# Sixteen expert tiles gathered inside the last attention group, twelve of them computed before the last routing results are in

## The chip, the cores and the metric

One core of one Trainium2 chip runs the whole program in one launch. The metric is the device time of a run in microseconds (us). Five engines work side by side, each through its own instructions in order: TensorE (PE, matmuls into the eight banks of the accumulator memory PS), VectorE (DVE), ScalarE (ACT), GpSimd (POOL) and SyncE (SP, which only issues DMAs here). They wait for each other on semaphores.

## What is computed

The reference embeds 4096 tokens (4 batches of 1024), adds one attention block and then a mixture of experts. Only the last part matters for the change:

```python
def _moe_forward(x, moe_router, moe_w13, moe_w2):
    router_logits = jnp.einsum('td,de->te', x_flat, moe_router)
    topk_logits, topk_idx = jax.lax.top_k(router_logits, TOP_K)        # 2 of 8 experts
    topk_weights = jax.nn.softmax(topk_logits, axis=-1)
    ...
    x_sort = x_flat[token_ids_sort]                                    # tokens sorted by expert
    w13_out = jax.lax.ragged_dot(x_sort, moe_w13, group_sizes)         # 256 -> 2 * 512
    gate, up = jnp.split(w13_out, [MOE_DIM], axis=-1)
    hidden = jax.nn.silu(gate) * up
    out_dispatch = jax.lax.ragged_dot(hidden, moe_w2, group_sizes)     # 512 -> 256
    out_flat = jnp.zeros_like(x_flat).at[token_ids_sort].add(out_dispatch * w_sort[:, None])
```

The attention ahead of it has 16 heads of width 16 (`softmax(p p^T / 4) p` with one projection p for queries, keys and values), an output projection, and a layer norm before each part.

## The kernel before

**Attention.** The work is cut into 16 groups of 256 tokens, four to a batch (`GROUPS`, `LAST = 15`). A group is 64 items: an item is one 128x512 block of scores. PE writes three items at a time (a unit) into banks 0 to 2 or 3 to 5 (`scores`), ACT takes the exponential of the whole unit (L758), and PE adds four items at a time (a quad, 16 to a group) into bank 6 (`sums`, L359). Between the quads of a group PE does the small products of the group before, at places that `after(quad)` lists: `fold`, `turn`, `tile_rows` (twice, L402 and L403), `rank`. DVE works on the same group a step later: `fold_out`, `place_blocks`, `copy_rows` (which gives back bank 7 to the second `tile_rows`), `choose` (the best two experts), `rank_read_out` and `places_out` (the place of each token in the list of its expert), `normalise` and `normal_rows` (the rows for the experts), `weigh`. So in group 15 the routing of group 14 is done, and places of group 13 are handed out at its start.

**Lists.** POOL writes each token's number into the slot that `places_out` gave it, in a table in HBM (`note`, 4 DMAs a group). An expert's list is cut into tiles of 128 slots; the work is always 68 tiles of 72 possible (`USUAL`, `ETILES`).

**Between the parts.** When group 15 has been summed, its own fold, turn, rows, choice and ranks follow one after the other (L379, L386, L414, L435), then `tiles_out` on DVE (which tile belongs to which expert), `normalise(15)`, `places_out(15)`, `last_slots`, the table gather on POOL (L709), `slot_table` on PE (L419, L421), `slots_out` (`idx_tok`, the tokens of every tile), `near_out` and `flags_out`. Twelve matmuls of no use (L626) run at the end. Only then POOL gathers the rows of tile 0 (L1421) and SP transposes them (L1400).

**Expert weights.** 24 pieces of 512 KB go through three raw buffers: SP loads piece n once the low half of piece n-3 is done, POOL or ACT casts its high half (L700, L732), POOL subtracts to get the low half (L631). 19 pieces are done beside the attention (`BESIDE`); pieces 19 to 23 lie where the exponentials were, so ACT casts them only after the last sum.

**Experts.** For tile j: `up` (12 matmuls of 512 columns, L1472), silu on ACT (L1522), weight and product on DVE (`hidden`, L1553), its two bfloat16 halves (`halved`, L1558 and L1560), a DMA transpose of these (L1405), `down` (12 matmuls of 256 columns, L1481), copy on ACT (L1527), and an adding scatter by POOL (L1438). PE does down(j) and then up(j+4), in a loop of four tiles. The scatter of tile m waits for scatter m-2.

## Time and profile before

| | us |
|---|---|
| median of 3 runs | 875.73 (874.70 to 876.11) |
| span of the profiled execution | 874.2 |
| last sum of the attention ends | 541.35 |
| first up begins | 579.18 |
| first down begins | 590.67 |
| thirteenth down begins | 639.85 |

The record gives the span of the profiled execution (first to last instruction) and no time of its own around it; 874.2 is 1.5 below the median of the runs. All times below are from the start of the span. A row of the timeline is a start, a duration, an engine, a line, an operation with its output and inputs, and a count; in brackets stands how long the engine had been idle and what released it. Rows of neighbouring equal instructions are merged, so the duration of a merged row covers all of them. Line numbers are those of the kernel before; L1472 and its like are written `PE L1472`.

### The profile page before, as it was taken

The page shows a single profiled execution, that of the slowest core. Times are in us where ns is not written, and L with a number is a line of the kernel's source. Part 1 is how long each engine was busy: PE and PEld are TensorE (multiplying, and loading weights), DVE is VectorE, ACT ScalarE, POOL GpSimd, SP SyncE. Part 2 cuts the span into 40 slices and gives each one's busy share as a digit, 9 for nine tenths or more (in the row PEclk, how much of TensorE's full clock was granted, in tenths as well). Part 3 has the DMA queues.
Part 4 walks back from the last instruction along what each step waited for, and adds up shares of the span by engine and source line. Part 5 has one row for each costly group of instructions (what it writes and reads, how often), then busy time and mean ns, then how long its engine had stood idle before and what let it go on. Part 6 is the DMA issues. An engine that isn't in the chain of part 4 may idle for free.

```text
span 874.2 us, 16623 instructions
## 1 busy us (share of the span) xinstructions
PE 767.1 (88%) x5249; PEld 300.0 (34%) x5250; DVE 510.9 (58%) x1623; ACT 544.6 (62%) x515; POOL 355.0 (41%) x305
## 2 busy tenths in 40 slices
PE   3699994999999999989999997289999999999992
PEld 1233220222222222222222221135555555555551
DVE  7644563576667558676756478654555555545540
ACT  0468993999989999989999997312222222222221
POOL 6760030302411330241133217256666666666652
PEclk9589996899999999999999999579999999999997
DMA  2030105012011101201110124349999999999973
GB/s 40 2 94 1 37 12 38 13 37 74 13 37 49 46 16 37 74 14 37 49 50 14 37 73 98 87 85 166 159 162 164 158 162 163 160 163 156 154 122 44
DMA packets 141362, 67.72 MB, mean 77 GB/s; under 512 B 114822, under 2 KB 136984, under 8 KB 141294
## 3 DMA queue, kind: packets, MB, share of 16 engines
q1 hardware_dynamic: 125262, 49.33, 27.5%
q0 software_dynamic: 16032, 17.55, 13.9%
q8 instruction: 35, 0.57, 0.4%
q14 instruction: 33, 0.27, 0.2%
HBM read 22.52 MB, written 17.57 MB: 46 GB/s over the span
## 4 chain that ended last, share of the span: by engine, by line
PE 69%; DVE 16%; ACT 5%; issue 5%; DMA 2%; another core or an unknown queue 1%; POOL 0%; SPq 0%; POOLq 0%; ACTq 0%; DVEq 0%
PE PS L359 20%; PE PS L1472 18%; PE PS L1481 10%; PE PS L347 9%; ACT shared L758 5%; PE PS L402 2%; PE PS L379 2%; DVE room L788 2%; DVE room L794 2%; PE PS L403 2%; DVE room L786 2%; PE PS L445 1%; DMA room<-room 1%; DVE room L790 1%
## 5 line engine op out<-in xcount | busy, mean ns | idle before, releaser
L758 ACT ACTIVATE shared<-PS 128x1536 f32<-128x1536 f32 x342 | 464.8, 1519 | 48.5 <-PE PS L347 36.3
L359 PE MATMUL PS<-shared,va 128*32 128x512 f32 x2048 | 279.8, 619 | 5.1 <-DVE room L1245 4.7
L637 POOL DMA_INDIRECT slots<-pair_no,room x60 | 59.5, 991 | 364.3 <-DVE room L917 350.6
L1472 PE MATMUL PS<-w_p,room 128*128 x816 | 186.7, 379 | 0.0
L347 PE MATMUL PS<-room,ak 32*128 32x512 bf16 x1024 | 137.5, 394 | 14.3 <-ACT shared L758 9.5
L1522 ACT ACTIVATE shared<-PS 128x512 f32<-128x512 f32 x68 | 40.6, 598 | 162.9 <-PE PS L1472 162.9
L1438 POOL DMA_INDIRECT out<-room,idx_tok x68 | 110.9, 1631 | 67.1 <-ACT room L1527 38.6
L1553 DVE SCALAR_TENSOR_TENSOR shared<-shared,room,PS 128x512 f32<-128x512 f32 x68 | 50.8, 748 | 124.5 <-ACT shared L1522 124.5
L1481 PE MATMUL PS<-shared,room 128*128 x816 | 101.1, 273 | 8.6 <-issue 5.9
L1472 PEld LDWEIGHTS PS<-w_p,room 128*128 128x128 f16 x816 | 79.8, 98 | 82.9 <-issue 0.6
L347 PEld LDWEIGHTS PS<-room,ak 32*128 32x128 bf16 x1024 | 33.5, 91 | 215.6 <-ACT shared L758 166.8
L1421 POOL DMA_INDIRECT room<-xrows,idx_tok x68 | 71.8, 1056 | 48.6 <-issue 28.2
L1481 PEld LDWEIGHTS PS<-shared,room 128*128 128x128 bf16 x816 | 76.2, 97 | 40.8 <-issue 27.0
L359 PEld LDWEIGHTS PS<-shared,va 128*32 128x32 f32 x2048 | 40.7, 109 | 67.2 <-issue 56.0
L1527 ACT COPY room<-PS 128x256 f32<-128x256 f32 x68 | 25.3, 372 | 61.5 <-PE PS L1481 60.8
L823 DVE COPY room<-PS 128x264 f32<-128x264 f32 x32 | 13.8, 433 | 65.8 <-PE PS L403 64.0
L1560 DVE TENSOR_TENSOR room<-shared,room 128x512 bf16<-128x512 f32 x67 | 46.4, 692 | 2.3
L1558 DVE CAST room<-shared 128x512 bf16<-128x512 f32 x67 | 35.0, 522 | 2.3
L644 POOL DMA_INDIRECT cw<-coeff,xi x32 | 31.1, 971 | 10.8 <-issue 9.3
L631 POOL TENSOR_TENSOR w_p<-room,w_p 128x1024 bf16<-128x1024 f32 x16 | 34.4, 2147 | 1.4
L786 DVE CAST room<-PS 128x512 bf16<-128x512 f32 x32 | 22.0, 688 | 18.5 <-PE PS L334 18.5
L794 DVE SCALAR_TENSOR_TENSOR room<-room,part_c 128x512 bf16<-128x512 bf16 x32 | 27.6, 861 | 1.1
(283 smaller groups left out, 616.2 us busy)
## 6 DMA issues: line engine op xcount, KB each, us to landing
room<-w SPq DMA_DIRECT2D x24, 512.0 KB, 4.9
xrows<-room SPq DMA_DIRECT2D x16, 258.0 KB, 3.2
out<-room SPq DMA_DIRECT2D x16, 256.0 KB
room<-room SPq DMA_TRANSPOSE x135, 4.1
room<-xrows,idx_tok POOLq DMA_INDIRECT x68
out<-room,idx_tok POOLq DMA_INDIRECT x68
slots<-pair_no,room POOLq DMA_INDIRECT x60
xT<-xT SPq DMA_DIRECT2D x3, 256.0 KB, 4.3
```

What stands on the lines that cost most here:

```text
L347: last = pe.matmul(PS[:, WIDE * (u % BUFS) + i, :], g.ak[r, k0:k0 + P], qf[r, grp % 2, 512 * c:512 * c + 512], start=True, stop=True)
L359: last = pe.matmul(PS[32 * slot:32 * slot + 32, ACC, :], g.va[:, KT * (grp // HG) + kt, c, :], prob[:, (4 * quad + slot) % (RING * WIDE), ...
L637: pool.indirect_dma_start(g.slots, bass.IndirectOffsetOnAxis(pos_i[:, grp % 2, 2 * k + kk:2 * k + kk + 1].bitcast(U32), 0), g.pair_no[:, t ...
L758: act.activation(prob[:, at:at + n, :].rearrange("p n q -> p (n q)"), PS[:, buf:buf + n, :].rearrange("p c q -> p (c q)"), ACT.Exp).then_i ...
L794: dve.scalar_tensor_tensor(qf[:, grp % 2, 512 * half:512 * half + 512], u2[:], g.part_c[:, 1:2], ures[:], ALU.mult, ALU.add).then_inc(qf_r ...
L1421: pool.indirect_dma_start(xs_w[:, j % XBUF, :], None, g.xrows, bass.IndirectOffsetOnAxis(g.idx_tok[:, j:j + 1].bitcast(U32), 0), bounds_ch ...
L1438: pool.indirect_dma_start(out, bass.IndirectOffsetOnAxis(g.idx_tok[:, m:m + 1].bitcast(U32), 0), y_s[:, m % XBUF, :], None, bounds_check=T ...
L1472: last = pe.matmul(PS[:, up_bank(k) + half, :], xsT[:, k, 2 * a + c, :], g.w13_p[:, w, c, ds(e, 1), FF * half:FF * half + FF].rearrange("p ...
L1481: last = pe.matmul(PS[:, YB[k % 2], 0:D], hidT[:, k, 4 * a + c, :], g.w2_p[:, w, c, ds(e, 1), :].rearrange("p e d -> p (e d)"), start=n == ...
L1522: act.activation(act_s[:], PS[:, up_bank(k), :], ACT.Silu).then_inc(silu_done, 1)
L1553: dve.scalar_tensor_tensor(hid[:], act_s[:], weight[:, k % 2:k % 2 + 1], PS[:, up_bank(k) + 1, :], ALU.mult, ALU.mult).then_inc(hid_ready, 1)
L1560: dve.tensor_tensor(halves[:, k, 1], hid[:], halves[:, k, 0], ALU.subtract).then_inc(hid_split, 1)
```

## The change

The order of the lists is used: after group 13 an expert's first n tiles are full, if it has n times 128 tokens, and nothing later changes them. The first 16 such tiles (`LEAD`) become tiles 0 to 15; the rest are numbered after them, so there are still 68.

- DVE: `lead_tiles` (24 small instructions) after `places_out(13)`, `lead_copy` before and `lead_slots` after `rank_read_out(14)`. The last routing chain is interleaved with `lead_hidden(0)` to `lead_hidden(11)`, four instructions each.
- POOL: `lead_rows` (gather of the table's 16 rows, then of the rows of tiles 0 to 3) goes ahead of `note(14)`; the low halves of pieces 19 to 23 and the gathers of tiles 4 to 7 are mixed; the last table gather comes after the gather of tile 7 and scatter 0. Scatters up to the sixteenth wait for the one before.
- PE: `lead_table` at quad 11 of group 15; `up` of tiles 0 and 1 on both sides of the last quad's sum; tiles 2 and 3 between fold, turn and rows; then twelve `lead_step`s (down(j), up(j+4)) with `rank(15)`, `slot_table` and the last flag product between them. The twelve matmuls of L626 are gone.
- ACT: silu of tiles 0 to 3 between the casts of pieces 19 to 23; the activations of `last_rows` and the exponential `gap_exp(15)` after silu(5).
- SP: the transposes of tiles 0 to 3 after the loads of pieces 19 to 21; piece 22 is loaded after the transpose of hidden tile 0, piece 23 after that of hidden tile 1.
- The tile buffers take the place of keys, queries, values and tokens of batches 0 to 2. For the case that everything has to be done again these are saved to HBM in groups 12 and 13 (four DMAs, 3.2 MB).
- The loop begins at tile 12 (`FIRST`), with the next gathers from tile 16 on.

```diff
+LEAD = 16
+CUT = GROUPS - 3
+KEPT = NBATCH - 1
...
             if initial and grp == CUT - 1:
+                keep_keys()
+            if initial and grp == CUT:
+                keep_tokens()
...
+        for n in range(BESIDE, BESIDE + WB):
             load(n)
-        store_x(GROUPS - 2)
-        store_h(GROUPS - 1)
-        store_x(GROUPS - 1)
+        for j in range(XBUF):
+            tiles_of.turn_x(sp, j, 0)
+        later = iter(range(BESIDE + WB, len(pieces)))
+        for j in range(LEAD - XBUF):
+            tiles_of.turn_hidden(sp, j % XBUF, j)
+            if j == 0:
+                store_x(LAST - 1)
+            for n in later:
+                load(n)
+                break
...
+            tiles_of.turn_x(sp, j % XBUF, j // XBUF + 1)
...
+        def lead_table():
+            pe.wait_ge(lead_copied, 1)
+            pe.wait_ge(rank_read, LAST)
+            pe.matmul(PS[:, UB, 0:LEAD], lead_f[:], g.ident[0:LEAD, 0:LEAD], start=True, stop=True).then_inc(lead_turned, 1)
...
+        def lead_step(j):
+            now, coming = tiles_of.expert(pe, j), tiles_of.expert(pe, j + XBUF)
+            if j == 0:
+                pe.wait_ge(w_lo, len(pieces))
+            if j == 1:
+                pe.wait_ge(rank_read, GROUPS)
+            tiles_of.wait_hidden(pe, j)
+            tiles_of.wait_rows(pe, j + XBUF)
+            tiles_of.down(pe, j % XBUF, j, now)
+            tiles_of.up(pe, j % XBUF, j + XBUF, coming)
...
+        pe.wait_ge(w_lo, W13)
+        pe.wait_ge(lead_ready, 3)
+        pe.wait_ge(exp_done, UNITS - 2)
+        tiles_of.wait_rows(pe, 0)
+        lead_up(0)
         while quad < ITEMS // 4:
             sums(quad)
             after(quad)
             quad += 1
+        tiles_of.wait_rows(pe, 1)
+        lead_up(1)
+        fold(LAST)
         last_residuals()
-        fold(LAST)
+        tiles_of.wait_rows(pe, 2)
+        lead_up(2)
         turn(LAST)
+        tiles_of.wait_rows(pe, 3)
+        lead_up(3)
         last_rows()
+        lead_step(0)
         rank(LAST)
+        for j in range(1, 6):
+            lead_step(j)
         slot_table()
+        lead_step(6)
+        lead_step(7)
...
-        for n in range(12):
-            pe.matmul(PS[:, 0, :], g.ones_b[:], g.ak[:, 0:512], start=True, stop=True)
+        for j in range(8, LEAD - XBUF):
+            lead_step(j)
...
+        def lead_rows():
+            for k in range(2):
+                pool.wait_ge(noted[k], 64 * ((CUT + 2 - k) // 2))
+            pool.wait_ge(lead_row_ready, 1)
+            pool.indirect_dma_start(lead_s[:], None, g.table,
...
+            for j in range(XBUF):
+                tiles_of.gather(pool, j)
...
             if grp == LAST:
+                lead_rows()
             if grp >= 1:
                 note(grp - 1)
-        for n in range(BESIDE, BESIDE + WB):
+        for n in range(BESIDE, len(pieces)):
             low(n)
+            if n == BESIDE:
+                tiles_of.lead_gather(pool, XBUF)
+            if n == BESIDE + 2:
+                tiles_of.lead_gather(pool, XBUF + 1)
+        for j in range(XBUF + 2, 2 * XBUF):
+            tiles_of.lead_gather(pool, j)
...
         act.wait_ge(summed, ITEMS // 4)
         act.wait_ge(w_hi, BESIDE)
-        for n in range(BESIDE, BESIDE + WB):
+        for j in range(XBUF):
+            high(BESIDE + j)
+            tiles_of.silu(act, j, j)
+        for n in range(BESIDE + XBUF, len(pieces)):
             high(n)
...
+        for j in range(LEAD - XBUF):
+            if j == 2:
+                last_rows()
+                gap_exp(LAST)
+            tiles_of.copy_y(act, j % XBUF, j)
+            tiles_of.silu(act, j % XBUF, j + XBUF)
```

On PE the end of group 15 stands so in the kernel before: L347 is `scores`, L359 `sums`, L408 the residual rows, L379 the fold, L386 the turn.

```order
L347 MATMUL PS<-room,ak 128x512 [waits exp_done]
L359 MATMUL PS<-shared,va 32x512 [waits exp_done]
L359 MATMUL PS<-shared,va 32x512 x3
L359 MATMUL PS<-shared,va 32x512 [waits exp_done]
L359 MATMUL PS<-shared,va 32x512 x3
L408 MATMUL PS<-resid,xT 128x264 x2
L379 MATMUL PS<-fold_sel,room 128x64 [waits rank_read,u_read,acc_copied]
```

The same place in the changed kernel, where L388 is `scores`, L400 `sums`, L1601 the load of the tile's expert and L1614 `up`:

```order
L388 MATMUL PS<-room,ak 128x512 [waits exp_done]
L400 MATMUL PS<-shared,va 32x512 [waits exp_done]
L400 MATMUL PS<-shared,va 32x512 x3
L1601 TENSOR_LOAD tile_expert [waits exp_done,xT_in0,lead_ready,w_lo]
L1601 ISA x2
L1614 ISA [waits hid_ready]
L1614 MATMUL PS<-w_p,ak 128x512
```

The last quad's sum, which came right behind the other, now stands behind the whole first `up`, and this waits for the transposed rows of tile 0.

On DVE, what follows `normal_rows(14)` in the changed kernel: L1401 copies the sums of group 15, L1641 to L1651 are the four instructions of a `lead_hidden`, L1051 to L1053 are `weigh(14)`, L908 and L912 `fold_out(15)`.

```order
L1401 TENSOR_SCALAR room<-PS 128x512 [waits a_summed]
L1641 TENSOR_SCALAR xq<-second,xq 128x1 [waits xT_in0]
L1644 SCALAR_TENSOR_TENSOR shared<-ak,xq,PS 128x512 [waits silu_done,weighed]
L1649 CAST xT<-shared 128x512 [waits hid_ready]
L1651 TENSOR_TENSOR xT<-shared,xT 128x512 [waits split_step]
L1051 TENSOR_SCALAR room<-room 128x2 [waits gap_done]
L1052 RECIPROCAL room<-room 128x2 [waits p_dve_step]
L1053 SCALAR_TENSOR_TENSOR room<-room 128x2 [waits p_dve_step]
L908 RECIPROCAL room<-PS 128x32 [waits folded]
L912 TENSOR_TENSOR room<-PS,room 128x4x16 [waits rden_step]
```

Before, the fold's instructions stood right behind the copy; now a `lead_hidden` and `weigh(14)` are between.

On SP the tail of the changed kernel: L268 loads a weight piece, L1565 transposes gathered rows, L1570 transposes a hidden tile, L278 stores rows.

```order
L268 DMA room<-w2 128x4x256 x3
L1565 DMA_TRANSPOSE ak<-xq 128x4x128 x4
L1570 DMA_TRANSPOSE va<-xT 128x8x128
L278 DMA xrows<-room 128x2x258
L268 DMA room<-w2 128x4x256
L1565 DMA_TRANSPOSE ak<-xq 128x4x128
L1570 DMA_TRANSPOSE va<-xT 128x8x128
L268 DMA room<-w2 128x4x256
```

Before, all five loads stood together ahead of every transpose; now the last two stand behind transposes of hidden tiles.

## Rows read from the trace of the kernel before

**Rows 1.** The page: 40 slices, TensorE busy, its granted clock, DMA share.

```profile
PE   3699994999999999989999997289999999999992
...
PEclk9589996899999999999999999579999999999997
DMA  2030105012011101201110124349999999999973
```

**Rows 2.** Windows: from, to, length, then busy of PE, PEld, DVE, ACT, POOL, clock, DMA.

```profile
541.35:579.18 37.83, 13.55 (x44) 7.81 (x45) 25.24 (x116) 8.40 (x12) 13.67 (x10) 0.55 0.41 88
...
590.67:639.85 49.18, 47.75 (x289) 27.51 (x289) 25.86 (x48) 11.31 (x24) 32.32 (x24) 1.00 0.97 164
```

**Rows 3.** Timeline of PE from the middle of group 15 to the first down.

```profile
525.93 0.71 PE L402 MATMUL PS<-resid,xT 73*128 73x264 f32 x2
...
534.52 0.39 PE L347 MATMUL PS<-room,ak 32*128 32x512 bf16 x3
...
540.28 1.07 PE L359 MATMUL PS<-shared,va 128*32 128x512 f32 x8 [0.45 <-ACT shared L758]
...
546.41 1.97 PE L379 MATMUL PS<-fold_sel,room 128*128 128x64 f32 x8 [3.97 <-DVE room L1245]
...
574.20 5.11 PE L626 MATMUL PS<-ak,ones_b 128*128 128x512 bf16 x12
579.18 10.53 PE L1472 MATMUL PS<-w_p,room 128*128 x48
590.67 1.50 PE L1481 MATMUL PS<-shared,room 128*128 x12 [0.96 <-DMA room<-room]
```

**Rows 4.** The window in which the granted clock rises again.

```profile
578.00:580.00 2.00, 2.00 (x8) 0.79 (x7) 0.27 (x1) 0.00 (x0) 2.00 (x2) 0.76 0.93 155
```

**Rows 5.** Timeline of DVE: copy of rows in group 15; `tiles_out`, end of `normalise(15)`.

```profile
524.78 0.43 DVE L823 COPY room<-PS 128x264 f32<-128x264 f32 x1 [0.70 <-PE PS L403]
...
555.89 0.17 DVE L928 TENSOR_TENSOR room<-room,expert_base 128x8 f32<-128x8 f32 x1
...
558.64 0.16 DVE L944 TENSOR_TENSOR room<-room,row_no 128x1 int32<-128x1 f32 x1
...
563.00 0.15 DVE L859 SCALAR_TENSOR_TENSOR room<-room 128x2 f32<-128x2 f32 x1
```

**Rows 6.** Timeline of POOL: weight halves and gathers.

```profile
533.34 2.14 POOL L631 TENSOR_TENSOR shared<-room,shared 128x1024 bf16<-128x1024 f32 x1
...
572.80 1.02 POOL L1421 DMA_INDIRECT room<-xrows,idx_tok  x1 [12.11 <-DVE idx_tok L962]
```

**Rows 7.** DMA issues of 520 to 600: count, KB each, median us to landing.

```profile
room<-w SPq DMA_DIRECT2D x5, 512.0 KB, 8.4
...
room<-slots,room POOLq DMA_INDIRECT x1, 2.6
```

**Rows 8.** The page: the same for the whole span.

```profile
room<-w SPq DMA_DIRECT2D x24, 512.0 KB, 4.9
```

**Rows 9.** Timeline of ACT: casts of pieces 20 and 21, change of tables.

```profile
546.09 1.04 ACT L732 CAST shared<-room 128x1024 bf16<-128x1024 f32 x1 [3.09 <-DMA room<-w]
549.70 1.04 ACT L732 CAST shared<-room 128x1024 bf16<-128x1024 f32 x1 [2.56 <-DMA room<-w]
...
565.11 1.28 ACT L776 ACT_TABLE_LOAD   x1
```

**Rows 10.** Timeline of DVE: the first hidden tile.

```profile
582.69 0.75 DVE L1553 SCALAR_TENSOR_TENSOR shared<-shared,room,PS 128x512 f32<-128x512 f32 x1 [3.21 <-ACT shared L1522]
...
583.47 0.60 DVE L1558 CAST room<-shared 128x512 bf16<-128x512 f32 x1
584.11 0.69 DVE L1560 TENSOR_TENSOR room<-shared,room 128x512 bf16<-128x512 f32 x1
```

**Rows 11.** Timeline: a small DVE operation beside a low half on POOL.

```profile
530.14 2.13 POOL L631 TENSOR_TENSOR shared<-room,shared 128x1024 bf16<-128x1024 f32 x1
530.15 2.16 DVE L837 TENSOR_TENSOR room<-room 128x16 bf16<-128x16 f32 x1
```

More of the change, by code:

```diff
@@ L570, in after @@
                 rank(grp - 1)
+            if at == 11 and grp == LAST:
+                lead_table()
             if at == 15 and preparing(grp, 1):
@@ L749, in first_tokens, with last_rows @@
             act.copy(g.ak[:, 0:S], PS[:, 2, :].bitcast(BF16)).then_inc(ak_copied, 1)
+        def last_rows():
+            act.wait_ge(scaled, 1)
+            for kk in range(2):
+                last = act.activation(xn[:, kk, :], h1s[:, LAST % 2, kk, 0:D], ACT.Identity, bias=mean[:, kk:kk + 1], scale=rstd[:, kk:kk + 1])
+            last.then_inc(halved, 1)
+            act.wait_ge(halved, 1)
+            act.copy(rows_h[:, LAST % 2, :, 0:D], xn[:]).then_inc(halved, 1)
         if initial:
@@ L1202, in vector @@
                 places_out(grp - 2)
+            if grp == LAST:
+                lead_tiles()
             if grp >= 1:
@@ L1281, in sync @@
     def sync(sp):
+        for there, here in ((g.ak[:, 0:S * KEPT], g.kept_ak), (g.xq[:, 0:S * KEPT], g.kept_xq), (g.xT[0:XROWS, 0:S * KEPT], g.kept_xT),
+                            (g.va[:, 0:KT * KEPT].rearrange("p t c r -> p (t c r)"), g.kept_va)):
+            sp.dma_start(there, here).then_inc(back, 16)
+        sp.wait_ge(back, 64)
         sp.wait_ge(zeroed, 2)
@@ new lines, in next_gather, with lead_gather, expert, wait_rows @@
+    def next_gather(pool, j, apart):
+        pool.wait_ge(weighed, j - XBUF + 1)
+        pool.wait_ge(up_mm, j - XBUF + 1)
+        gather(pool, j)
+        if j >= XBUF + 3:
+            scatter(pool, j - XBUF - 3, apart)
+    def lead_gather(pool, j):
+        if j == XBUF:
+            pool.sem_inc(y_free, XBUF + 1)
+        next_gather(pool, j, 1)
+    def expert(pe, j):
+        return pe.value_load(g.tile_expert[0:1, one(j + 1)], min_val=0, max_val=E - 1)
+    def wait_rows(pe, j):
+        pe.wait_ge(xT_in[j % XBUF], 16 * (j // XBUF) + 16)
@@ new lines, in down, with silu @@
+    def down(pe, k, j, e):
+        pe.wait_ge(y_copied, j + 1)
+        terms = [(c, a, w) for c in range(4) for a, w in ((0, 0), (0, 1), (1, 0))]
+        for n, (c, a, w) in enumerate(terms):
+            last = pe.matmul(PS[:, YB[k % 2], 0:D], hidT[k][:, 4 * a + c, :],
+                             g.w2_p[:, w, c, ds(e, 1), :].rearrange("p e d -> p (e d)"),
+                             start=n == 0, stop=n == len(terms) - 1)
+        last.then_inc(y_mm, 1)
+    def silu(act, k, j):
+        act.wait_ge(up_mm, j + 1)
+        act.wait_ge(hid_ready, j + FREE)
+        act.activation(act_s[:], PS[:, up_bank(k), :], ACT.Silu).then_inc(silu_done, 1)
@@ L1578, in tower @@
+    x.rows, x.turn_x, x.turn_hidden, x.gather, x.lead_gather = rows, turn_x, turn_hidden, gather, lead_gather
+    x.expert, x.wait_rows, x.wait_hidden, x.up, x.down, x.silu, x.copy_y, x.hidden, x.halved = expert, wait_rows, wait_hidden, up, down, silu, copy_y, hidden, halved
+    x.sync, x.gpsimd, x.vector, x.scalar, x.tensor = sync, gpsimd, vector, scalar, tensor
+    return x
 def tower(nc, ins, out):
```

416 lines of the change are left out of this document (236 added, 180 removed).

## The prediction

> **What bounds the kernel now.** I read the page first [rows 1]: PE is busy 9 tenths and at full clock nearly everywhere, except in slices 25 to 27 (546 to 612 us), where both digits fall. The windows [rows 2] size that hole: in the 37.8 us between the last sum and the first up PE is busy 13.6 us at a mean clock of 0.55, and 5.1 us of that are the twelve idle-work matmuls [rows 3]. Behind it PE is the bound: 47.8 of 49.2 us busy for twelve tiles, 4.10 us each, at clock 1.00. DVE is busy 25.2 of the 37.8, and the fold's wait of 3.97 ends with it [rows 3]. So the hole is a chain of small DVE steps with small products between, and the `up`s that follow, 2.63 us each (10.53/4), need none of it for tiles whose lists are known. The small products are 13.55 - 5.11 = 8.4 us at a mean clock of 0.55, so 4.6 at the full one. An ideal fill would bring the first up from 579.18 to 541.35 + 4.6 and save the wait of 0.96 ahead of the first down: 34 us.
>
> I compare at one mark that both kernels have: the start of down(12), 639.85 before (590.67 + 49.18 [rows 2]). From there on both do the same 56 tiles in the same loop.
>
> **The change part by part.**
>
> *DVE in group 15.* `lead_tiles` has 24 instructions. The 17 first are like L928 to L944, 2.9 us; seven more at 0.17 to 0.2 us make 4.2 us [rows 5]. They stand in front of the copy at 524.78, which PE's second `tile_rows` waits for, and behind this `scores` stands. The copy comes at about 528.5, the second `tile_rows` at 529.0 instead of 525.93. ACT is the bound of the attention, and its next unit depends on these scores: +3.1 us.
>
> *lead_table.* POOL's second low half ends at 535.48 [rows 6]; the gather of 16 rows is issued at 535.8 and has landed after 2.6 [rows 7], 538.4; copy and `rank_read_out(14)` 0.8: 539.2. In the order it stands behind the scores that began at 534.52 [rows 3]; PE would be there at 534.9 + 3.1 = 538.0. So +1.3: the sum before the last ends at about 544.3.
>
> *Rows of tile 0.* `lead_slots` gives the tokens at 540.2. Before, 6.4 us lay between the gather's start (572.80) and the first up (579.18) [rows 3, 6]: 546.6. But SP has the loads of pieces 19 to 21 ahead of the transposes, and the last of these was in only at 549.70 [rows 9], 0.6 later now, since SP waits for `weigh(13)`; with about 1.1 for the transpose behind it: 551.4. These are the two ends. Nothing in the rows says to which of them the transposes are nearer; I take the middle, 549.1.
>
> In the Trainium skill, "DMA: Bandwidth & Descriptors", section "Queues, rings and completion order", descriptors of one ring are consumed in order on each DMA engine. By that rule the transposes sit behind piece 21 and the first up is at 551.4, which would make the final time 2.3 us more than mine. No run here yet shows loads and transposes together.
>
> *Ups.* PE will have been idle for some 5 us by then, and after such gaps it stood at the lower of its two levels (1.2 and 2.4 GHz). The twelve fillers of 512 columns took 5.11 there, where the twelve of an up took 2.63 after the clock had risen (0.76 in the window 578 to 580) [rows 3, 4]. So I count 5.1 for the first up: it ends at 554.2, and the last sum at 555.3 (+1.07). Before, it was over at 541.35. **ACT's casts of pieces 19 to 23 wait for this sum**, and `lead_step(0)` waits for the last low half. That is the path, and it runs:
>
> - cast 19, silu(0): 555.3 + 1.03 + 0.6 = 557.0. Product of tile 0: 557.8.
> - The halves are SBUF operations beside POOL's low half 19 (556.3 to 558.4). In [rows 11] a DVE operation of 0.2 us took 2.16, as long as POOL's. So they start at 558.4, and `hidden(0)` is ready at 559.6 (0.5 + 0.7 [rows 10]).
> - `weigh(14)` stands next, and the low halves 20 and 21 run back to back from 559.8. It gets through at 561.9 and ends at 562.5. SP's store of rows waits for it, and load 22 is behind the store: issued 562.6.
> - fold_out, product and halves of tile 1: 562.5 + 1.1 + 0.3 + 0.8 + 1.2 = 565.9; SP transposes it (1.2), then issues load 23: 567.2. It lands 4.9 later [rows 8], 572.1; cast 1.0, low 2.1: **575.2**.
>
> The cover of PE until then is 549.1 + 5.1 + 1.1 + three ups 7.9 + 2.9 of small products + about 2 of waits on DVE = 568.1. PE idles some 7 us.
>
> *Twelve steps.* 12 x 4.10 = 49.2. Again 2.5 for the half clock. The rest of the small products (ranks, table, flag) 4.6 - 2.9 = 1.7. Waits: `up(j)` needs product j-2, and DVE does `tiles_out` 3.1 and `normalise(15)` 4.4 [rows 5] one behind the other; up(7) waits 1.2. ACT does the exponential of group 15 between two silus, which means two loads of tables (the order has them) at 1.28 [rows 9]; with `last_rows` it makes silu(6) late by about 3, and up(8) and up(9) wait 3.8 for the products of tiles 6 and 7. Together 5. Sum: 575.2 + 49.2 + 2.5 + 1.7 + 5.0 = **633.6**.
>
> The Trainium skill, "ScalarE: Activation LUTs", section "What ACT_TABLE_LOAD costs", counts about 2.66 us for a switch with its drain. The row has 1.28, and I take it; by the page's figure for both switches the time would be up to 2.7 more.
>
> *At nothing.* The saved copies: four DMAs, 3.2 MB, on SP's queue in groups 12 and 13. The DMA engines are 0 to 2 tenths busy in slices 18 to 22 [rows 1], and the loads and stores behind them have a group (32 us) of room. Without that cover each would be later by the copies' some 10 to 20 us, and the attention with it by nothing until a buffer is missing. Scatters one behind the other instead of two: pitch in the steps is above 4 us, a scatter's issue 1.6. The loop and its tail are unchanged. Straight-line steps instead of a loop save the branch, 0.4 every four tiles: up to -1.8, at the low end only.
>
> **Sum.** 639.85 - 633.6 = 6.2 us less, span 868.0. With the 1.5 between span and median: **869.5**.
>
> **Rivals.**
>
> *The path is shorter (faster still).* If the rows come at 546.6 (-2.5), the DVE halves and `weigh` are not held by POOL (-2.7), and the steps have no branch (-1.8), and the clock stays up at the first down (-2.5), the time is 860.0; any two of them give about 865. For it: each is a cost that I took from one row and laid on a place where the two engines may just miss each other. Against it: the four are independent, and the chain is long enough for each slip to be made good by another wait.
>
> *The transfers are slow, and the kernel is slower.* Three DMAs stand on the path one behind the other: the rows of tile 0, load 22 or 23, and the transpose of a hidden tile ahead of its down. The loads of this stretch took 8.4 us in the median, against 4.9 over the span [rows 7, 8]. In the changed kernel gathers, transposes, stores and loads meet. At +3.5 for each of the three the path is 10.5 longer: 880.0. It decides from 6.2 us of extra landing on. For it, the 8.4; against it, that median comes from three loads in a row, and 22 and 23 are now alone.
>
> *No gain of note.* DVE paces the steps: between rank and last flag it has 18.8 us of routing and eight tiles of 2.3 us, 37 us for PE's 52. If each wait for a silu or an up cannot be filled, because the order is fixed, six more us are lost, and the time is 875.5. The point is where half of the twelve ups wait 1 us more than I counted.
>
> **How the numbers follow.** Forecast (867 to 873) 0.45; shorter path (under 867) 0.33; no gain 0.12; slow transfers 0.10. Eight in ten lie from 861 to 878. A measurement tells about 0.2%, 1.8 us, from no change. Faster by more, under 874.0: the first two and a small part of the third, 0.82. Within: most of the third, 0.09. Slower: 0.09.
>
> **What would show it.** In the profile after: the copy of rows in group 15 at 528 to 529, the first up at 546.6 to 551.4 with about twice the time of the others, the cast of piece 19 within 0.2 of the last sum, near 555; the last low half at 575, with an idle PE of some 7 us before the first down; ups waiting for DVE's product around steps 3 to 5; 4.1 us a tile from the loop on. It is wrong if the last low half isn't what the first down waits for, or if the steps take over 5 us each throughout, or if the loop's pitch has changed.

## The result, and the profile after

| | kernel before | kernel changed |
|---|---|---|
| median | 875.88 us (874.7 to 876.11, 4 runs) | 891.38 us (887.02 to 896.6, 4 runs) |
| profiled execution, span | 874.2 us | 887.9 us (time 889.64) |
| ratio | | 1.018, 95% interval 1.015 to 1.022 |

The change made the kernel 1.8% slower. I had forecast 869.5 us, with a range of 861 to 878.

The times of the kernel before differ between chips (medians of 874 to 892 us in the comparisons below), so every experiment is given as a ratio to runs of the kernel before on its own chip. Of four of the kernels below one run each was in a slower state (over 1.5% above the fastest); the ratios leave it out, the medians don't. A ratio and its interval stand as they are on record and aren't the quotient of the two medians: for the control below the ratio is 0.986, the medians give 0.992.

The page of the changed kernel, 40 slices: TensorE busy, its granted clock, DMA share, and the second line of the chain that ended last. It answers to [rows 1].

```profile
PE   3699996999899999989999975878788999999992
...
PEclk9589996999999999999999987789999999999997
DMA  1030103112101111110321124457788999899973
...
PE PS L400 19%; PE PS L1614 14%; PE PS L388 9%; PE PS L1623 8%; ACT shared L864 5%; DMA out<-xT,idx_tok 5%; PE PS L443 2%; DMA ak<-xq 2%; DVE room L895 2%; DVE room L901 2%; PE PS L444 2%; DVE room L893 1%; PE PS L420 1%; DMA xq<-xrows,idx_tok 1%
```

The deep hole of before (slices 25 to 27, with a 2 in it) is gone. In its place stands a wide shallow one, eight slices of 5 to 8. And the chain has a new member, the scatters of expert rows into the output (`out<-xT,idx_tok`).

Windows of the changed kernel: start of the last sum but one to first down, the twelve steps, the next twelve tiles, the rest (columns as in [rows 2]).

```profile
541.89:580.72 38.83, 21.25 (x81) 8.96 (x83) 22.85 (x57) 10.45 (x14) 18.71 (x14) 0.72 0.43 100
580.72:646.24 65.52, 53.67 (x296) 30.34 (x303) 39.92 (x132) 15.07 (x29) 31.77 (x24) 0.93 0.72 119
646.24:703.61 57.37, 50.05 (x283) 27.73 (x289) 25.22 (x48) 11.86 (x25) 35.42 (x27) 0.97 0.92 144
703.61:872.00 168.39, 162.58 (x980) 95.74 (x1000) 87.23 (x162) 40.65 (x85) 106.92 (x79) 1.00 0.94 153
```

A tile costs 65.52/12 = 5.5 us in the steps and 57.37/12 = 4.8 in the twelve tiles behind them, where [rows 2] has 4.10. Most of that is idle time of PE: 50.1 busy of 57.4. The rest is its clock: behind the wait of 2.85 at 640.72 the down takes 2.74 and not 1.50. Timeline of PE, at the first up, the first down, and from tile 11 on (at the end of a row: idle time before it, and what ended it).

```profile
553.07 4.90 PE L1614 MATMUL PS<-w_p,ak 128*128 x11 [10.11 <-issue]
557.90 1.38 PE L400 MATMUL PS<-shared,va 128*32 128x512 f32 x8
...
580.72 2.74 PE L1623 MATMUL PS<-shared,va 128*128 x12 [4.16 <-POOL shared L709]
...
640.72 2.74 PE L1623 MATMUL PS<-shared 128*128 x12 [2.85 <-issue]
...
646.24 1.50 PE L1623 MATMUL PS<-shared,va 128*128 x12
...
656.16 1.50 PE L1623 MATMUL PS<-shared,va 128*128 x12 [1.61 <-DMA ak<-xq]
```

The late `down`s wait for transposed rows, hence for gathers (a step waits ahead of down(j) for the rows of tile j+4). The reason is in the chain of waits of the same kernel, 600 to 720 us (start, us, what):

```profile
609.92 0.92 POOL xq L1573
610.84 0.71 issue
611.76 5.83 DMA out<-xT,idx_tok
617.64 0.56 issue
618.41 3.83 DMA out<-xT,idx_tok
622.30 0.70 issue
623.22 4.98 DMA out<-xT,idx_tok
628.25 0.70 issue
629.16 5.40 DMA out<-xT,idx_tok
...
655.82 2.90 issue
659.68 2.88 DMA xq<-xrows,idx_tok
662.63 3.81 DMA ak<-xq
666.57 1.62 PE PS L1623 x12
```

From 611.8 to 654.2 the chain holds nothing but scatters: one lands, 0.8 to 1.0 us later POOL begins to issue the next (617.59 to 618.41), and it lands 3.8 to 5.8 after that. Only behind that does the chain go back through a gather and a transpose to PE. POOL's own timeline has the same, and its end:

```profile
640.03 1.97 POOL L1584 DMA_INDIRECT out<-xT,idx_tok  x1 [1.69 <-DMA out<-xT,idx_tok]
...
645.39 1.58 POOL L1584 DMA_INDIRECT out<-xT,idx_tok  x1 [2.04 <-DMA out<-xT,idx_tok]
...
650.16 1.58 POOL L1584 DMA_INDIRECT out<-xT,idx_tok  x1 [1.83 <-DVE xq L1641]
...
679.68 1.58 POOL L1584 DMA_INDIRECT out<-xT,idx_tok  x1 [0.31 <-issue]
...
682.93 1.58 POOL L1584 DMA_INDIRECT out<-xT,idx_tok  x1 [0.30 <-issue]
```

Five us from scatter to scatter, then, from tile 17 on, 3.25. Tiles 0 to 16 are those whose scatter waits for the landing of the one before it, because the test for neighbouring tiles that share a token covers only the later ones. The first scatter and the 17th are 65.4 us apart in the kernel before and 91.7 in the changed one.

### The profile page after: what moved, and what is told of

Same layout as the page of the kernel before. It is cut to its first block, busy times and chain, and to the rows that moved or that the text cites. A ratio compares the mean times of both kernels' runs of the same rounds, so it can differ in the third digit from the quotient of the medians.

```text
span 887.9 us, 16506 instructions
## 1 busy us (share of the span) xinstructions
PE 768.0 (86%) x5190; PEld 300.2 (34%) x5240; DVE 516.3 (58%) x1652; ACT 547.0 (62%) x517; POOL 356.1 (40%) x306
## 4 chain that ended last, share of the span: by engine, by line
PE 59%; DVE 16%; DMA 8%; issue 7%; ACT 6%; another core or an unknown queue 2%; POOL 1%; POOLq 0%; SPq 0%; ACTq 0%; DVEq 0%
PE PS L400 19%; PE PS L1614 14%; PE PS L388 9%; PE PS L1623 8%; ACT shared L864 5%; DMA out<-xT,idx_tok 5%; PE PS L443 2%; DMA ak<-xq 2%; DVE room L895 2%; DVE room L901 2%; PE PS L444 2%; DVE room L893 1%; PE PS L420 1%; DMA xq<-xrows,idx_tok 1%
## 5 line engine op out<-in xcount | busy, mean ns | idle before, releaser
L400 PE MATMUL PS<-shared,va 128*32 128x512 f32 x2048 | 281.7, 623 | 9.3 <-DVE room L1401 9.3
L1614 PE MATMUL PS<-w_p,ak 128*128 x782 | 193.0, 392 | 16.3 <-issue 10.1
L388 PE MATMUL PS<-room,ak 32*128 32x512 bf16 x1024 | 137.8, 395 | 19.1 <-ACT shared L864 10.8
L1584 POOL DMA_INDIRECT out<-xT,idx_tok x68 | 110.8, 1629 | 81.7 <-ACT xT L1636 29.4
L1631 ACT ACTIVATE ak<-PS 128x512 f32<-128x512 f32 x68 | 40.6, 597 | 153.5 <-PE PS L1614 138.1
L1644 DVE SCALAR_TENSOR_TENSOR shared<-ak,xq,PS 128x512 f32<-128x512 f32 x68 | 50.8, 748 | 121.6 <-ACT ak L1631 119.4
L1614 PEld LDWEIGHTS PS<-w_p,ak 128*128 128x128 f16 x816 | 81.8, 100 | 104.7 <-issue 27.0
L388 PEld LDWEIGHTS PS<-room,ak 32*128 32x128 bf16 x1024 | 33.6, 91 | 218.0 <-ACT shared L864 165.2
L1623 PE MATMUL PS<-shared,va 128*128 x612 | 77.3, 277 | 17.5 <-issue 6.5
L1573 POOL DMA_INDIRECT xq<-xrows,idx_tok x68 | 72.3, 1063 | 40.8 <-issue 27.0
L1623 PEld LDWEIGHTS PS<-shared,va 128*128 128x128 bf16 x612 | 57.4, 98 | 42.4 <-issue 31.9
L400 PEld LDWEIGHTS PS<-shared,va 128*32 128x32 f32 x2048 | 40.9, 109 | 71.6 <-issue 54.8
L1651 DVE TENSOR_TENSOR xT<-shared,xT 128x512 bf16<-128x512 f32 x67 | 46.4, 693 | 2.3
L1649 DVE CAST xT<-shared 128x512 bf16<-128x512 f32 x67 | 34.8, 519 | 2.3
L709 POOL TENSOR_TENSOR w_p<-room,w_p 128x1024 bf16<-128x1024 f32 x16 | 34.5, 2154 | 1.4
```

The costliest lines, as they stand in the source:

```text
L388: last = pe.matmul(PS[:, WIDE * (u % BUFS) + i, :], g.ak[r, k0:k0 + P], qf[r, grp % 2, 512 * c:512 * c + 512], start=True, stop=True)
L400: last = pe.matmul(PS[32 * slot:32 * slot + 32, ACC, :], g.va[:, KT * (grp // HG) + kt, c, :], prob[:, (4 * quad + slot) % (RING * WIDE), ...
L1573: pool.indirect_dma_start(xs_w[:, j % XBUF, :], None, g.xrows, bass.IndirectOffsetOnAxis(g.idx_tok[:, j:j + 1].bitcast(U32), 0), bounds_ch ...
L1584: pool.indirect_dma_start(out, bass.IndirectOffsetOnAxis(g.idx_tok[:, m:m + 1].bitcast(U32), 0), y_s[:, m % XBUF, :], None, bounds_check=T ...
L1614: last = pe.matmul(PS[:, up_bank(k) + half, :], xsT[:, k, 2 * a + c, :], g.w13_p[:, w, c, ds(e, 1), FF * half:FF * half + FF].rearrange("p ...
L1623: last = pe.matmul(PS[:, YB[k % 2], 0:D], hidT[k][:, 4 * a + c, :], g.w2_p[:, w, c, ds(e, 1), :].rearrange("p e d -> p (e d)"), start=n == ...
```

## The experiments

"Before" and "changed" are the two kernels; a kernel's median stands with that of before on the same chip.

**Two scatters in flight.** One of the three call sites of tiles 0 to 16; the other two are changed alike:

```diff
-        next_gather(pool, j, 1)
+        next_gather(pool, j, 2)
```

> Scatters of tiles 0 to 16 wait for the one before the last instead of the last, as those of the later tiles do. That drops the guard for inputs in which two neighbouring tiles hold the same token. Theory A (chain of scatters): in the trace of the changed kernel a scatter begins 5 us after the one before while they are serial (629.16, 635.40, 640.03, 645.39, 650.16) and 3.2 us after it once they are not (679.68, 682.93, 686.17), PE takes 4.10 a tile; if that pitch starves PE, the steps 5 to 11 and the loop's tiles 12 to 23 come back to 4.1 to 4.5 us each, and the time falls by 7 to 14 us, to 877 to 884. Theory D (the DMA engines are simply full, and the gathers are late whatever the scatters wait for): the scatters issue earlier and land later, the time moves by less than 2 us. First up and first down stay where they are (553, 581) in both.

878.94 us against 884.76, ratio 0.993 (0.989 to 0.997). The windows of the twelve steps and the twelve tiles behind:

```profile
582.64:642.03 59.39, 51.45 (x296) 29.91 (x303) 40.40 (x133) 15.67 (x30) 35.69 (x27) 0.96 0.84 140
642.03:691.49 49.46, 47.51 (x282) 27.39 (x289) 24.78 (x47) 11.44 (x24) 31.56 (x24) 1.00 0.94 157
```

59.4 and 49.5 where the changed kernel has 65.5 and 57.4, so 14.0 us less in these 24 tiles, and from the first up to the first down 27.4 as against 27.7. The DMA engines are busier, not less (0.84 for 0.72), so they weren't what held the scatters: theory D is out, A stands. Of PE's waits in the steps most of what is left, 4.7 us in three, is for DVE's products.

**The change again, on another chip.** 

> The changed kernel as it is, on the same chip and against the same runs of the kernel before as the other kernels here. It was 1.018 of the kernel before, and with the scatters two apart 0.993, but not on the same chip. Theory A (serial scatters): it is again 1.013 to 1.022 here, so the difference belongs to the kernel. If the two measurements differ because the chips do, it comes out below 1.005 here.

890.39 against 880.53: 1.011 (1.007 to 1.016). Slower on both, by 10 to 16 us.

**The suspect alone, in the kernel before.**

```diff
-                    scatter(j - XBUF - 3, apart)
+                    scatter(j - XBUF - 3, 1 if j - XBUF - 3 <= 16 else apart)
```

> The kernel before with nothing moved, only its scatters of tiles 0 to 16 made to wait for the one before, as the changed kernel does. Theory A: the chain of the changed kernel shows 4.9 us from one of these scatters to the next (5.83, 3.83, 4.98, 5.40, 3.81 to landing and 0.6 to 0.7 between) where PE needs 4.10; 17 times 0.8 is 13.6 us, less what the buffers cover at first (gathers run seven tiles ahead, some 3 to 5 us): 6 to 14 us slower than before, ratio 1.007 to 1.016. Theory F (it takes the stretch of the last attention, with its routing on DVE and its loads, to make the scatters late; in the plain loop they would keep up): the same time as before within 2 us.

895.23 against 880.53, the same chip as the run above: 1.016 (1.011 to 1.020), 14.7 us for an edit that moves nothing. That is a little more than the 6 to 14 that I expected. PE waits for rows in the plain loop too (timeline of PE):

```profile
648.19 1.50 PE L1481 MATMUL PS<-shared,room 128*128 x12 [1.35 <-DMA room<-room]
...
659.14 1.50 PE L1481 MATMUL PS<-shared,room 128*128 x12 [1.95 <-DMA room<-room]
```

Its first 17 scatters span 81.55 us, 5.10 from one to the next, where before has 65.39/16 = 4.09. 16 x 1.01 is 16, and 14.7 was measured: the buffers cover next to nothing.

**All 68 of them.** The same kernel, with `run(USUAL, 1)` for `run(USUAL, 2)`. 

> The kernel before with all 68 scatters made to wait for the one before. Theory A: four times as many tiles at 4.9 us for 4.1: 68 times 0.8 is 54 us, less the 3 to 5 that the gathers cover at first: 40 to 55 us slower, ratio 1.045 to 1.062, PE's pitch 4.7 to 4.9 throughout. Theory F: in the plain loop the scatters keep up, the pitch stays at 4.1 and the ratio is under 1.01.

956.41 against 880.53: 1.084 (1.077 to 1.092). 75.9 us, beyond what I expected (1.045 to 1.062): the 67 steps from the first scatter to the last take 340.9 us (601.79 to 942.66), 5.09 each, where the kernel before has 268.3, 4.00 each. That is 72.6 of the 75.9. I had counted 4.9 and 4.10. Four times the tiles, five times the loss.

**Rows of tile 0 ahead of two loads.** In SP's program, on the changed kernel:

```diff
-        for n in range(BESIDE, BESIDE + WB):
-            load(n)
+        load(BESIDE)
         for j in range(XBUF):
             tiles_of.turn_x(sp, j, 0)
+        for n in range(BESIDE + 1, BESIDE + WB):
+            load(n)
```

> SP issues the four transposes of gathered rows behind the load of piece 19 and ahead of the loads of pieces 20 and 21, instead of behind all three. Theory B (the rows of tile 0 queue behind the loads): the first up comes at 547 to 549 instead of 553.1, the last sum with it, cast 19 and the last low half too unless the later loads 20 and 21 hold them: first down 3 to 6 us earlier, time 3 to 6 us less. Theory E (what holds the rows is the issue on SP itself, 5.3 us for the first transpose in the changed kernel, because the gather of tile 0 has not landed): the first up stays within 1 us of 553 and the time within 1 us, or is worse, since loads 20 and 21 now stand behind it and the low halves wait for them.

893.16 against 884.76: 1.011 (1.006 to 1.015), like the changed kernel. From the first gather to the first up it was 7.8 us (547.17 to 555.00), with the order unchanged on the same chip 7.9 (547.34 to 555.25). Theory B found nothing to win there. The two aren't quite alike, as the gather began 5.5 us behind the first load here and 6.7 there; and the edit wasn't tried where the interval is long, see below.

**The last sum ahead of the first up.** PE's last `sums` and `after` moved above `lead_up(0)`.

> PE does the last sum of the attention before the first up instead of behind it. Theory C (the last sum releases ACT's casts of pieces 19 to 23, and the chain of these sets the first down): the last sum comes at 545 instead of 557.9, cast 19 at 546.5 instead of 559.4, the low halves follow at the pace of POOL (2.1 us each, pieces 22 and 23 by their loads), the routing of group 15 starts 13 us earlier, and the first down comes 5 to 10 us before 580.7; the time falls by 4 to 9 us. Theory A (the serial scatters pace everything behind the first down): the first down comes earlier but the serial scatters take 5 us a tile from there, and less than half of the gain is left at the end. If first up and its rows are the path, nothing changes.

889.67 against 884.76: 1.004 (1.001 to 1.008). The matmuls of the last sum end 3.8 us ahead of the first up, and the first down came at 583.21, 31.7 behind the start of the last sum but one (33.2 with the order unchanged on the same chip). That gain of 1.5 us is not the 5 to 10 of theory C, but the run is no fair test of it, as the release of the casts hardly moved. The sum's matmuls end at 554.38, yet these two start together at 560.96:

```profile
560.96 1.05 ACT L829 CAST shared<-room 128x1024 bf16<-128x1024 f32 x1 [4.81 <-remote]
...
560.96 0.69 DVE L1400 TENSOR_SCALAR room<-PS 128x512 f32<-128x512 f32 x1 [4.42 <-remote]
```

DVE's copy of the sums needs no weight, only the last sum. Load 19 was issued at 544.62, and the loads of this stretch took 5.5 us to land. So it isn't the piece that was late, but the sum's semaphore, whose last update the trace has at 560.94, 6.6 us behind the end that it gives the matmuls. Why stays open. The cast came 9.4 us behind the start of the last sum but one, against 11.8 with the order unchanged. By its ratio this kernel is 6 to 12 us faster than the changed one (1.011 and 1.018 on other chips), which is more than the 1.5 us explain; that stays open too. Pieces 22 and 23 were as late as ever. The chain of waits of this kernel says why:

```profile
558.22 4.07 PE PS L1613 x11
562.32 0.60 ACT ak L1630
563.03 0.76 DVE shared L1643
...
565.23 4.48 DVE room L1050
...
570.13 0.37 SPq L278
570.55 4.64 DMA room<-w
575.22 1.06 ACT shared L829
```

Up, product, halves, then `weigh(14)` held for 4.48 us beside two low halves on POOL; the store of rows on SP waits for it, and load 22 stands behind the store. These low halves come after the cast at 560.96, so a release that really came early might have spared `weigh(14)` the hold; no run without the weights ahead shows that.

**All of these, and the weights ahead.** Scatters two apart, rows first, sum first, and in addition: ACT casts pieces 19 to 21 ahead of `silu(0)`, SP issues loads 22 and 23 ahead of `turn_hidden(0)`, POOL does its low halves ahead of the gathers of tiles 4 to 7 (all but the last, which comes behind the gather of tile 4). 

> The three edits together (scatters two apart, transposes ahead of loads 20 and 21, last sum ahead of the first up), and besides ACT casts pieces 19 to 21 ahead of the silu of tile 0, SP issues loads 22 and 23 ahead of the transpose of hidden tile 0, POOL does low halves before the gathers of tiles 4 to 7. If the loss is the sum of these causes, the first down comes 10 to 15 us before 580.7, the steps take 4.1 to 4.6 each, and the time is 862 to 870, under the kernel before. If the DMA engines or DVE's routing pace the stretch instead, the steps stretch by what the first down gained, and the time stays over 880.

874.96 against 884.76: 0.989 (0.985 to 0.993). The steps take 56.9, but the first down came at 582.35, 31.9 behind the last sum but one. That gained 1.3 us and not 10, and the time is neither of the two that I had named: with rows first, loads 20 and 21 were late for POOL (load 20 was issued at 556.66 and took 9.60).

**The same without rows first.** The heart of it, SP's program:

```diff
-        later = iter(range(BESIDE + WB, len(pieces)))
+        for n in range(BESIDE + WB, len(pieces)):
+            load(n)
         for j in range(LEAD - XBUF):
             tiles_of.turn_hidden(sp, j % XBUF, j)
```

> On the changed kernel: scatters two apart, the last sum ahead of the first up, ACT casting pieces 19 to 21 ahead of the silu of tile 0, SP issuing the loads of pieces 22 and 23 ahead of the transpose of hidden tile 0, POOL doing its low halves ahead of the gathers of tiles 6 and 7; the transposes of rows stay behind loads 19 to 21. Theory G (what holds the first down is the chain up(0), product, halves, store of rows, load 22, cast, load 23, cast, low half; moving the sum alone could not shorten it): the first down comes when PE has done its four ups and last rows, 5 to 8 us earlier against the last sum but one than with the scatters alone (33 us there), and the time is 4 to 8 us under that kernel, ratio 0.984 to 0.989. Theory H (the loads themselves are slow beside gathers and notes, 16 us for piece 19, and moving them forward only moves the wait): the first down gains less than 2 us and the ratio is that of the scatters alone, 0.993.

869.01 against 880.53: 0.986 (0.982 to 0.990). Theory G: the first down comes 27.4 us behind the last sum but one. It no longer waits for a weight, but 1.11 us for the transposed rows of tile 4, whose gather (571.80) stands behind the low halves on POOL; the rest is PE's own work. ACT, SP and PE of this kernel:

```profile
559.33 2.94 ACT L825 CAST shared<-room 128x1024 bf16<-128x1024 f32 x3 [4.65 <-remote]
...
562.61 2.46 SPq L268 DMA_DIRECT2D room<-w  x2
...
577.41 1.50 PE L1619 MATMUL PS<-shared,va 128*128 x12 [1.11 <-DMA ak<-xq]
```

The 16 us of theory H for piece 19 are the time from the issue of load 19 to its cast in the kernel above (544.62 to 560.96), not to its landing; load 19 of this kernel landed 5.5 us after its issue. Here too the cast of piece 19 starts 6.5 us behind the end of the last sum (552.86).

**Three variants of that kernel, on a third chip.** Itself again as the control, without the saves of keys and tokens, with the serial scatters back, and with the sum behind the first up.

> The control, on the same chip: scatters two apart, last sum ahead of the first up, weights ahead. It was 0.986 of the kernel before, interval 0.982 to 0.990; if that belongs to the kernel it comes out in 0.980 to 0.991 again.

> The kernel with scatters two apart, the last sum ahead of the first up and the weights ahead (ratio 0.986), without the four saves of keys and tokens to memory in groups 12 and 13 and without DVE's wait for them; the second pass over the tokens, which this input doesn't need, would then find nothing saved. My forecast costed the saves at nothing. If so, the same time as the control beside it within 1.5 us. Theory K (3.2 MB on SP's queue make the loads and stores behind them late, or slow the attention): 2 to 10 us faster, and the last sum of the attention that much earlier.

> The same kernel with the saves, but with the scatters of tiles 0 to 16 waiting for the last one again, as in the changed kernel. Theory A: the price of the serial scatters was 14.7 us on the kernel before and some 13 to 20 on the changed one; here it is again 12 to 18 us over the control, and PE's steps 5 to 16 stretch to 5 us. The time is then 1.000 to 1.007 of the kernel before: the new order alone, with the guard kept, brings back about half of what the changed kernel lost, and no gain. Rival (an earlier first down gives the scatters a start, so that they have less to catch up): under 8 us over the control.

> The same kernel as the control, but with the last sum behind the first up again, as in the changed kernel: weights and scatters changed alone. Theory G' (with loads 22 and 23 no longer behind the store of rows, the casts set the first down, and these wait for the last sum): cast 19 comes behind the up, 560 instead of 559, since load 19 landed only at 559 in the kernel with both: the two agree within 1 us and the sum's place is worth nothing. Theory C (the sum's place was worth the 5.9 us): 4 to 6 us slower than the control.

| against before (892.20) | us | ratio |
|---|---|---|
| control | 885.06 | 0.986 (0.981 to 0.992) |
| no saves | 880.05 | 0.983 (0.979 to 0.988) |
| serial scatters | 896.52 | 1.004 (1.000 to 1.008) |
| sum behind | 884.10 | 0.987 (0.982 to 0.991) |

The serial scatters cost 0.0179 x 892.2 = 16.0 us here too by the ratios, 11.5 by the medians; in the profiled executions it is 306.7 us from the first down to the end against the control's 289.6, so 17.1. A first down that comes earlier gives them no start, so the rival is out. Without the saves the median is 5.0 us lower and the ratio 0.003, with intervals that overlap: that decides neither for nothing nor for theory K. The traces tell more. SP's queue without the saves, and in the control:

```profile
430.34 0.38 SPq L273 DMA_DIRECT2D out<-room  x1
...
485.86 0.38 SPq L273 DMA_DIRECT2D out<-room  x1
```

```profile
432.90 0.38 SPq L273 DMA_DIRECT2D out<-room  x1
...
442.38 0.37 SPq L310 DMA_DIRECT2D kept_ak<-ak  x1
...
470.18 0.29 SPq L318 DMA_DIRECT2D kept_xT<-xT  x1
...
488.43 0.40 SPq L273 DMA_DIRECT2D out<-room  x1
```

55.52 us for two groups without the four saves, 55.53 with them. The 2.6 us between the two were there before the first save. The saves cost nothing in groups 12 and 13. From the last of these marks to the start of the last sum but one it is 74.3 us without them and 76.8 to 77.0 in the three profiles with them on this chip. But kernels that all have the saves lie as far apart there on one chip (73.5 and 76.1; 74.3 to 77.9), so these 2.5 us can be put down to the saves no more than they can be ruled out. The place of the sum can't be told from its medians; from the first up to the first down it was 22.8 us with the sum behind and 21.6 with it ahead. The landing of load 19 at 559 that theory G' goes by is, again, the time of its cast.

**The guard kept, and cheap.** A token goes to an expert once, so two tiles of one expert share none. A wait is needed only where the expert turns. DVE writes the differences of the tiles' experts, and POOL branches on them:

```diff
-        if m >= 1 and apart == 1:
+        if 1 <= m < LEAD:
+            turned = pool.value_load(g.turn[0:1, m:m + 1], min_val=0, max_val=E - 1)
+            with pool.If(turned > 0):
+                pool.wait_ge(y_out[(m - 1) % 2], 16 * ((m - 1) // 2 + 1))
+        elif m >= 1 and apart == 1:
             pool.wait_ge(y_out[(m - 1) % 2], 16 * ((m - 1) // 2 + 1))
```

> The changed kernel with that one edit, the wait only where the expert turns, and nothing else moved. It was 1.018 and 1.011 of the kernel before with sixteen waits and 0.993 with none. Theory A': 0.990 to 0.997, a gain of the size that was forecast (0.993). Rival (branches as dear as waits): 1.000 or more.

869.91 against 873.98: 0.995 (0.993 to 0.997). This is the changed kernel with that one edit. Its steps take 58.1 and the twelve tiles behind them 51.7, where it was 59.4 and 49.5 without any guard: what is left of the waits isn't free. No run shows how many turns there were among the sixteen tiles.

> The kernel with the last sum ahead of the first up and the weights ahead, and with the guard kept for every input: a scatter waits for the one before it only where the two tiles belong to different experts (a token goes to an expert once, so tiles of one expert never share a token), decided by a branch on POOL, and at tile 16 always. Sixteen tiles of some seven full ones an expert have two or three such turns. Theory A' (the number of serial waits in a row decides, at 0.9 us each, and POOL catches up at 3.3 us a tile behind each): the ratio is that of the kernel without the guard, 0.986, within 0.003, and under 1 all over its interval. Rival (a branch on POOL costs as much as the wait that it saves): the scatters are 4.5 us apart or more, and the ratio is 0.992 to 1.004.

862.01 against 873.98: 0.989 (0.985 to 0.993), the best kernel that keeps the guard for every input, 1.1% under before. The windows of its twelve steps and the twelve tiles behind:

```profile
568.37:625.37 57.00, 50.07 (x303) 28.59 (x303) 43.65 (x146) 15.68 (x30) 34.33 (x27) 1.00 0.93 156
625.37:675.26 49.89, 48.28 (x288) 27.41 (x289) 24.58 (x48) 11.09 (x24) 32.48 (x24) 1.00 0.96 158
```

No step has to pay for the branches: 57.0, as without any guard (57.1 and 57.0). The rival, a branch as dear as a wait, is out. In this profile the cast of piece 19 came 1.9 us behind the last sum, not 6.5, and the first down was 28.5 us behind the last sum but one, no sooner than the 27.4 above: with the weights ahead, an early release of the casts brings nothing. The kernel wasn't run on other inputs, with more turns among the sixteen tiles.

## Why the prediction was wrong, point by point

The forecast at its marks, and the profiled execution of the changed kernel. Its attention ran 3.4 us ahead of before's from about group 4 on, before anything that the change touches; I carry this as a term of its own.

| term | forecast | trace | adds |
|---|---|---|---|
| attention up to group 15 | 0 | 3.4 earlier | -3.4 |
| first up | 549.1 | 553.07 (556.5 on before's clock) | +7.4 |
| first up to first down | 26.1 | 27.65 | +1.5 |
| twelve steps | 58.4 | 65.5 | +7.1 |
| from down(12) to the end | 234.4 | 241.7 | +7.3 |
| span | 868.0 | 887.9 | +19.9 |

- **At nothing: the scatters. This step failed, and the sign with it.** I wrote "pitch in the steps is above 4 us, a scatter's issue 1.6" and took the one for cover of the other. What a serial scatter is waiting for is the landing of the one before, not its issue. The page of before has no landing time for the scatters; its nearest rows were the loads' 4.9 [rows 8] and a gather's 2.6 [rows 7]. With 4.9, and the 0.8 to 1.0 that the chain above has from landing to next issue, the cycle would be some 5.8, over PE's 4.1 [rows 2]; with 2.6 it would be hidden. A cost that these rows bound between 0 and 17 x 1.7 = 29 us doesn't stand "at nothing". And I need not have gone by such bounds, for the trace of the kernel before has the landing where its last scatters are waited for, in the chain and in POOL's timeline:

```profile
854.21 4.48 DMA out<-room,idx_tok
...
859.56 1.54 POOL L1438 DMA_INDIRECT out<-room,idx_tok  x1 [0.93 <-DMA out<-room,idx_tok]
```

One landed 4.48 us after its issue began, and 0.87 later the next was issued: 5.35, or 1.25 over PE's pitch, some 21 us for 17 tiles. The cost measured 14.7 us alone in the kernel before, 16.0 in the improved one, and by ratios (1.018 or 1.011 against 0.995) 14 to 21 in the changed one. It accounts for the last two terms of the table: together they are 307.2 us, forecast 292.8, and 292.3 with the scatters two apart (304.7 and 307.0 in the two profiles with serial scatters on that chip).

- **"The loop and its tail are unchanged"** failed for the same reason. Four of the serial tiles are scattered in the loop, and it starts with POOL behind: waits of 1 to 2 us for rows on to the down of tile 20 (686.73).
- **Steps: the sum held once the scatters were out of it.** 58.4 forecast; 59.4 with the scatters two apart, 58.1 with the guard at the turns. The half clock of the first down is there (2.74 us, then 1.50), and so are the waits of ups for products: 4.7 us in three with the scatters two apart, where I had 5.0 in all. Both table loads between the silus took 1.28 us, as summed (599.56 and 601.34), and the next activation began 0.02 us behind the first.
- **Rows of tile 0: off, and out of my range.** 13.6 us from the gather to the first up in the profiled execution, where my two ends were 6.4 and 11.2. The gather itself came 2.7 us later than forecast on before's clock (542.9 for 540.2). The chain there has the gather landing in 5.19 and the transpose in 6.81. In eleven of the other twelve profiles that have this piece it was 7.3 to 9.8, about the value I took (8.9); in one it was 14.1. The loads seem to be part of it: where the gather began over 6 us behind the issue of loads 19 to 21 the interval was 7.3 to 7.9 (three profiles), where it began 4.3 to 5.2 behind, 8.7 to 9.8 (six). But the two long ones have 4.1 and 5.1, so something else adds 4 to 5 us there, and it stays open. The rule of the Trainium skill that I weighed at this place ("DMA: Bandwidth & Descriptors", section "Queues, rings and completion order") isn't settled either: with the transposes ahead of loads 20 and 21 the interval was 7.8 in both profiles, the gather 5.5 and 6.3 us behind load 19, and with them behind all three it was 7.9 at 6.7.
- **First up to first down: right in its length, and by the path told.** In the changed kernel the cast of piece 19 came 0.1 us behind the last sum; the first up took 4.90 (forecast 5.1) and the first down waited for the last low half (L709). Single terms were off: `weigh(14)` beside two low halves took 4.48, where I had 2.3 until it got through; PE idled 4.2 and not 7.
- **The saves at nothing: right in groups 12 and 13,** 55.53 and 55.52 us; up to 2.5 us in the groups behind them are not ruled out.
- **The rivals.** I had given the slow transfers 0.10, with the rows, a load and a transpose on the path. The transfer that decided is in none of them: the scatter wasn't on my list of DMAs on the path, since I had struck it off one part earlier. The size of the whole change without this fault was right: forecast -6.2 us, 0.993; measured 0.993 with the guard off and 0.995 with it kept at the turns. That isn't luck of two faults that cancel: with the guard off its parts lie within 2 us of the forecast, 33.2 us from the last sum but one to the first down (forecast 32.0), 59.4 for the steps (58.4), 232.8 from there to the end (234.4).

## What to carry to other kernels

When a queue goes from two in flight to one, its cycle is the landing time plus all that its engine does between landing and next issue; set that against the consumer's pitch. Where the page gives no landing time, look in the trace for a place where something waited for such a transfer (here the tail of the kernel before); only where there is none, bound it by the nearest transfers and keep both ends. A guard that is made static "for a few tiles" is paid on each of them: ask what condition it stands for, and branch on that if it is rare. And before moving the work that a chain seems to wait for, follow the in-order queue of each DMA issuer: here two loads stood behind a store that had nothing to do with them. And when an engine waits, ask which of its waits was the last to end, and whether another engine was let go at the same moment.

## What the runs showed of the hardware

- A scatter of 128 rows with accumulation landed 3.8 to 5.8 us after POOL began to issue it (eight in the chain of the changed kernel; 4.48 at the tail of the kernel before), and one at a time they came 5.1 us apart over a whole loop of 68.
- In these rows a DVE operation of 0.2 us that starts beside POOL's TENSOR_TENSOR on SBUF lasts until POOL is done, and for two of them back to back it lasts through both: 4.48 us (L1050 and L1051), for 2.16 beside one in [rows 11]. Not every DVE operation is held: the product that reads PS (L1644, 561.01 in the changed kernel) took its usual 0.76 us beside a low half on POOL (560.49 to 562.61).
- A branch on POOL on a value from SBUF, at tiles 1 to 15, left POOL's cycle at 3.24 to 3.27 us where it was quickest (tiles 5 to 7 of the last kernel), against 3.25 with no branch (from tile 17 on in the changed kernel).
- The semaphore of a sum can come well behind the end that the trace gives its matmuls, here 6.4 us (two scatters in flight, sum first, weights ahead) and 6.6 us (sum first) in profiles from two chips, against 0.05 in the changed kernel's; both engines that waited for it started with it.
